# Weights taken with a step of two, moving columns and PSUM bank run through backwards, in a graph-convolution and LSTM kernel

## The reference

```
h   = item_feat @ W_item.T + b_item                 # 10000 x 128
b   = layernorm(x) @ W_user.T + b_user
x1  = x + relu(adj @ h + b)                          # adj is 10000 x 10000, fp32
y   = lstm(layernorm(x1))                            # 10000 steps, hidden size 128
out = x1 + 2*y + prefix*fw_att + suffix*bw_att       # running sums of y gated by a two-way logit
```

## Time and profile before

| | us |
|---|---|
| median of 3 runs | 1426.8 (1426.69 to 1429.94) |
| the profiled execution | 1429.61 |
| its span, first to last instruction | 1427.8 |
| stage one, block 0 (first pass to tail pass) | 10.0 to 86.9 |
| stage one, blocks 1 to 19 | 86.9 to 1125.8 |

### The profile page before, as it was taken

How to read it: one execution, slowest core, us unless ns; L and a number is a source line. 1 busy time by engine, 2 the same in 40 slices (tenths; PEclk the granted TensorE clock), 3 DMA queues, 4 the chain that set the end, 5 groups by cost and what they waited for, 6 DMA issues and landing times.

```text
span 1427.8 us, 26195 instructions
## 1 busy us (share of the span) xinstructions
PE 1401.8 (98%) x7438; PEld 1210.5 (85%) x7438; DVE 1273.0 (89%) x2102; ACT 1056.4 (74%) x1449; POOL 213.4 (15%) x189
## 2 busy tenths in 40 slices
PE   8999999999999999999999999999999999999995
PEld 7888888888888888888888888888888899999995
DVE  7999999999999999999999999999999766676667
ACT  5677787777877877877877877877877676556663
POOL 0000000001001001001001001001000132036776
PEclk9999999999999999999999999999999999999998
DMA  9999999999999999999999999999999303000003
GB/s 373 344 336 382 399 387 392 394 385 383 405 385 395 391 387 397 392 382 402 384 387 402 391 377 405 387 380 402 388 388 382 133 1 144 0 2 0 0 0 145
DMA packets 143466, 442.96 MB, mean 310 GB/s; under 512 B 23944, under 2 KB 43337, under 8 KB 143307
## 3 DMA queue, kind: packets, MB, share of 16 engines
q1 hardware_dynamic: 126048, 426.43, 76.7%
q10 hardware_dynamic: 17387, 16.14, 4.0%
HBM read 432.15 MB, written 10.36 MB: 310 GB/s over the span
## 4 chain that ended last, share of the span: by engine, by line
PE 93%; DVE 5%; ACT 0%; issue 0%; DMA 0%; POOL 0%; ACTq 0%; DVEq 0%
PE psG L882 24%; PE psG L883 24%; PE psG L884 24%; PE psZ L980 10%; PE psZ L966 3%; PE psZ L968 3%; PE psZ L970 3%; DVE a_lo L1201 2%; PE psZ L986 1%; PE psT L857 1%; PE psI L930 1%; DVE item_lo L1234 1%; DVE u L1516 1%; DVE u L1215 0%; PE psG L875 0%
## 5 line engine op out<-in xcount | busy, mean ns | idle before, releaser
L665 ACT ACTIVATE a_hi<-raw 128x1000 fp32r<-128x1000 f32 (+1 forms) x800 | 819.5, 1030 | 241.9 <-PE psG L884 212.7
L1201 DVE TENSOR_TENSOR a_lo<-raw,a_hi 128x1000 fp32r<-128x1000 f32 (+1 forms) x800 | 897.8, 1171 | 22.9 <-ACT a_hi L665 19.9
L882 PE MATMUL psG<-a_hi,item_hi 128*128 128x500 f32 x1560 | 611.3, 392 | 2.3 <-DVE a_lo L1201 1.4
L883 PE MATMUL psG<-a_lo,item_hi 128*128 128x500 f32 x1560 | 606.0, 388 | 0.0
L884 PE MATMUL psG<-a_hi,item_lo 128*128 128x500 f32 x1560 | 604.6, 388 | 0.0
L882 PEld LDWEIGHTS psG<-a_hi,item_hi 128*128 128x128 f32 x1560 | 293.5, 188 | 65.5 <-DVE a_lo L1201 3.5
L884 PEld LDWEIGHTS psG<-a_hi,item_lo 128*128 128x128 f32 x1560 | 293.1, 188 | 59.5
L883 PEld LDWEIGHTS psG<-a_lo,item_hi 128*128 128x128 f32 x1560 | 293.7, 188 | 55.5
L980 PE MATMUL psZ<-hist,wh 128*128 (+1 forms) x1264 | 167.1, 275 | 2.9 <-DVE hist L1354 2.2
L980 PEld LDWEIGHTS psZ<-hist,wh 128*128 128x128 f32 x1264 | 154.0, 191 | 3.8 <-issue 2.4
L466 POOL TENSOR_TENSOR row_terms<-var,minus_half 125x4 f32<-125x4 f32 x20 | 37.6, 1878 | 677.9 <-DVE var L1152 677.9
(11 more groups left out here) (186 smaller groups left out, 857.1 us busy)
## 6 DMA issues: line engine op xcount, KB each, us to landing
raw<-in_adj_main SPq DMA_DIRECT2D x760, 500.0 KB, 6.6
raw<-in_adj_main SPq DMA_DIRECT2D x40, 250.0 KB, 4.7
sq<-rstd_copy ACTq DMA_DIRECT2D x20, 250.0 KB, 7.0
u<-x_copy SPq DMA_DIRECT2D x1, 5000.0 KB, 14.4
x_copy<-x_rows SPq DMA_DIRECT2D x19, 250.0 KB, 7.2
sq<-rows_copy ACTq DMA_DIRECT2D x19, 250.0 KB, 5.3
un_bb<-rows_copy ACTq DMA_DIRECT2D x19, 250.0 KB, 7.6
u<-in_itemT SPq DMA_DIRECT2D x9, 512.0 KB, 8.0
```

The lines of the kernel that those rows point to most:

```text
L665: nc.scalar.activation(a_hi[:, s % CUT, 0:n], raw[:, r % RAW, at:at + n], ACT.Copy)\
L882: pe.matmul(bank, w_hi, hi, start=(c == 0), stop=False)
L883: pe.matmul(bank, w_hi, lo, start=False, stop=False)
L1201: last = dve.tensor_tensor(a_lo[:, s % CUT, 0:m], raw[:, r % RAW, at:at + m], a_hi[:, s % CUT, 0:m].bitcast(f32), ALU.subtract)
```

## The change

The item parts are stored in pairs of chunks: in each 256 columns the even ones belong to the first chunk, the odd ones to the second, so that a chunk's weights are 128 columns with a step of two. The item matmul L930 writes `psI` in that order, and the bias `bi` is doubled (each element twice), so that the elementwise steps stay as wide as they were. The passes of L882 to L884 read their moving slices from the last column to the first and write the bank from the last column to the first; L875 and the three bias passes stay forwards. The room for the wider `bi` comes from `inv_rows` and `item_tail`, which become parts of `x1_rows`, and five small tiles (`moments`, `mean_sum`, `mean_gap`, `gap_sq`, `spread`) stand between the large ones. Worked out as above, `item_hi` stays at 69440, `item_lo` comes to 110016, `a_hi` to 182560 and `a_lo` to 198560. Stage two is untouched.

```diff
+PAIR = 2 * HID
...
-        inv_rows = sb("inv_rows", [2, P])
...
-        bi = sb("bi", [P, HID])
+        bi = sb("bi", [P, 2 * HID])
...
         item_hi = sb("item_hi", [P, (CH + 1) * HID], f32r, first)
-        item_tail = sb("item_tail", [P, STACKED], f32, first)
+        moments = sb("moments", [SW, SUB, 6], f32, first)
+        mean_sum = sb("mean_sum", [SW, SUB], f32, first)
         item_lo = sb("item_lo", [P, (CH + 1) * HID], f32r, first)
         raw = sb("raw", [P, RAW, MAXC * BW], f32, first)
+        mean_gap = sb("mean_gap", [SW, SUB], f32, first)
+        gap_sq = sb("gap_sq", [SW, SUB], f32, first)
+        spread = sb("spread", [SW, SUB], f32, first)
...
+        item_tail = x1_rows[:, 2 * HID:2 * HID + STACKED]
+        inv_rows = x1_rows[0:2, 3 * HID:4 * HID]
...
+        def item_cols(c):
+
+            return slice(c // 2 * PAIR + c % 2, (c // 2 + 1) * PAIR, 2) if c < CH else slice(c * HID, (c + 1) * HID)
...
                 bank = psG[:, par, 0:BW]
+                back = bank[:, ::-1]
...
-                            hi = a_hi[:, s % CUT, i * BW:(i + 1) * BW]
-                            lo = a_lo[:, s % CUT, i * BW:(i + 1) * BW]
-                            w_hi = item_hi[:, c * HID:(c + 1) * HID]
-                            w_lo = item_lo[:, c * HID:(c + 1) * HID]
-                            pe.matmul(bank, w_hi, hi, start=(c == 0), stop=False)
-                            pe.matmul(bank, w_hi, lo, start=False, stop=False)
-                            last = pe.matmul(bank, w_lo, hi, start=False, stop=False)
+                            hi = a_hi[:, s % CUT, i * BW:(i + 1) * BW][:, ::-1]
+                            lo = a_lo[:, s % CUT, i * BW:(i + 1) * BW][:, ::-1]
+                            w_hi = item_hi[:, item_cols(c)]
+                            w_lo = item_lo[:, item_cols(c)]
+                            pe.matmul(back, w_hi, hi, start=(c == 0), stop=False)
+                            pe.matmul(back, w_hi, lo, start=False, stop=False)
+                            last = pe.matmul(back, w_lo, hi, start=False, stop=False)
...
+            def quad_cols(c):
+                k = c % 4
+                return slice(k // 2 * PAIR + k % 2, (k // 2 + 1) * PAIR, 2) if c < CH else slice(k * HID, (k + 1) * HID)
...
-                    last = pe.matmul(psI[0:rows, q % 2, (c % 4) * HID:(c % 4 + 1) * HID], columns, wi[:, :],
+                    last = pe.matmul(psI[0:rows, q % 2, :][:, quad_cols(c)], columns, wi[:, :],
...
-                                      bi[:, :].unsqueeze(1).to_broadcast([P, n, HID]), ALU.add)\
+                                      bi[:, :].unsqueeze(1).to_broadcast([P, n // 2, PAIR]), ALU.add)\
...
-            dve.tensor_copy(bi[:, :], psW[:, 0:HID]).then_inc(bi_ready, 1)
+            dve.tensor_copy(bi[:, :].rearrange("p (h e) -> p h e", e=2),
+                            psW[:, 0:HID].unsqueeze(2).to_broadcast([P, HID, 2])).then_inc(bi_ready, 1)
```

More of the change, by code:

```diff
@@ L35 @@
 STACKED = STACK[-1] + TAIL
+PAIR = 2 * HID
+assert CH % 2 == 0
 PIECES = 20
@@ L143, in program @@
         total = sb("total", [P, 1])
-        wd, dfd = wi, bi
+        wd, dfd = wi, bi[:, 0:HID]
         first = ExitStack()
         item_hi = sb("item_hi", [P, (CH + 1) * HID], f32r, first)
-        item_tail = sb("item_tail", [P, STACKED], f32, first)
+        moments = sb("moments", [SW, SUB, 6], f32, first)
+        mean_sum = sb("mean_sum", [SW, SUB], f32, first)
         item_lo = sb("item_lo", [P, (CH + 1) * HID], f32r, first)
         raw = sb("raw", [P, RAW, MAXC * BW], f32, first)
+        mean_gap = sb("mean_gap", [SW, SUB], f32, first)
+        gap_sq = sb("gap_sq", [SW, SUB], f32, first)
+        spread = sb("spread", [SW, SUB], f32, first)
         a_hi = sb("a_hi", [P, CUT, HALF * BW], f32r, first)
@@ L166, in program @@
         v = un_bb[:, 0:BW]
[L167 to L171, removed]
         var = sb("var", [SW, SUB], f32, first)
@@ L874, in body @@
                             if c == CH:
-                                last = pe.matmul(bank, item_hi[0:STACKED, c * HID:(c + 1) * HID],
+                                last = pe.matmul(bank, item_hi[0:STACKED, item_cols(c)],
                                                  a_hi[0:STACKED, s % CUT, i * BW:(i + 1) * BW], start=False, stop=True)
                                 continue
-                            hi = a_hi[:, s % CUT, i * BW:(i + 1) * BW]
-                            lo = a_lo[:, s % CUT, i * BW:(i + 1) * BW]
-                            w_hi = item_hi[:, c * HID:(c + 1) * HID]
-                            w_lo = item_lo[:, c * HID:(c + 1) * HID]
-                            pe.matmul(bank, w_hi, hi, start=(c == 0), stop=False)
-                            pe.matmul(bank, w_hi, lo, start=False, stop=False)
-                            last = pe.matmul(bank, w_lo, hi, start=False, stop=False)
+                            hi = a_hi[:, s % CUT, i * BW:(i + 1) * BW][:, ::-1]
[5 more added lines that the diff above has]
+                            last = pe.matmul(back, w_lo, hi, start=False, stop=False)
                         last.then_inc(halves_done, 1)
@@ L1214, in item_sum_part @@
                     dst = u[:, L + 4 * q * P:L + (4 * q + n) * P]
-                    dve.tensor_tensor(dst.rearrange("p (c h) -> p c h", h=HID),
-                                      psI[:, q % 2, 0:n * HID].rearrange("p (c h) -> p c h", h=HID),
-                                      bi[:, :].unsqueeze(1).to_broadcast([P, n, HID]), ALU.add)\
+                    dve.tensor_tensor(dst.rearrange("p (c h) -> p c h", h=PAIR),
+                                      psI[:, q % 2, 0:n * HID].rearrange("p (c h) -> p c h", h=PAIR),
+                                      bi[:, :].unsqueeze(1).to_broadcast([P, n // 2, PAIR]), ALU.add)\
                         .then_inc(item_sum, 1)
@@ L1222, in item_sum_part @@
                 dve.wait_ge(prep, 1)
[L1223 to L1226, removed]
+                pair, single = slice(0, PAIR), slice(PAIR, PAIR + HID)
+                for part, a, b in ((pair, 0, P), *((single, a, a + TAIL) for a in STACK)):
+                    dve.tensor_tensor(sq[a:b, part], psI[a:b, q % 2, part],
+                                      bi[a:b, :] if part is pair else bi[a:b, 0:PAIR:2], ALU.add)\
                         .then_inc(item_sum if a == STACK[-1] else prep, 1)
```

## The result

The change makes the kernel slower: 1438.55 us median (1437.33 to 1439.22, 4 runs) against 1427.6 for the kernel before beside it (4 runs), ratio 1.0075 with a 95% interval of 1.0061 to 1.0089, some 11 us. The prediction of 1404 had it faster, and the result lies outside its range. The profiled execution took 1437.87, its span is 1436.1, 8.3 more than before.

The account below looks back on a forecast made before the run. The prediction took TensorE to bound the blocks, with VectorE and DMA within 5%. Blocks 1 to 19 at -25 us and block 0 at +2 on a span of 1427.8 gave 1404.8, so a median of 1404; range 1380 to 1430.

Parts of the forecast that it names:

- Side by side they should meet once and part: Stage one's passes: weight and slice reads, both running downwards at one speed, would meet once, cutting 226.5 ns to 213.
- the 213 ns: Predicted time of a stage-one pass after the change, from 226.5, with 208 as the lower bound; TensorE needs 51.4 us a block.
- it comes once per pass: Claim that a TensorE pass's loss, 18 ns at 500 columns, comes once per pass, as the weight load does.
- hardly grows with the columns: Claim on TensorE passes: the loss is 12 ns at stage two's 256 columns and 18 ns at stage one's 500.
- Rival A: Stage one's passes stay as they are, so only block 0's +2 us remains: 1427 to 1429 us; chance 0.17.
- Rival C: Stage one's weight loads with a step of two take longer: passes some 246 or 300 ns, +93 or +350 us; chance 0.17.
- the 38 to spare: Slack in ns of a stage-one weight load: it lasts 188 within a pass of 226.5, and beyond that it decides.
- stage two 0: Stage two keeps its code and addresses, so its time was to change by 0.
- bound 0.3: Copy to the doubled `bi`, on the path of the first quad in block 0: at most +0.3 us.
- low end of its bounds: Block 0's step-two writes of `psI` by the item matmul: bounds 0 and +21 us, taken as +4.
- the DMA as the next bound: Blocks 1 to 19, once passes are faster: DMA sets 53.3 us a block, 1.3 less, -25 us over 19 blocks.
- floors of 52.6 to 54.2: DMA time per block, in us, behind the forecast's own span of 1392 to 1419 us; chance 0.52.

Follow-up runs that it names:

- e5: Kernel of TensorE passes alone with other lengths, a repeated column and 64 pairs of weight and slice places: 13 pairs settle at 220.0 ns, the rest at 223 to 229.
- e4: Kernel of TensorE passes alone, tiles at the addresses of the kernel before, 48 passes per form: 226.0 ns as before, 228.6 as after.
- e6: Passes alone, one weight place and 16 slice places, for backwards, step two and both: none settles at 220 ns; backwards 226.7 at 11 of 16.
- e11: e10 with the slices and the bank of the three passes run through backwards: 1432.41 us, ratio 1.0025.
- e8: The kernel before with 384 of 500 columns in the passes of L882 to L884, all but a block's first: 1404.3 us, blocks of 53.41 us.
- e9: Passes alone at the addresses of e7, 48, then other passes or nothing, then 48 more: 220 ns with nothing between, 226 to 233 after one of 64 columns.
- e2: The changed kernel with slices and bank forwards again, step of two and new tile places kept: 1433.15 us, ratio 1.0035.
- e1: The kernel before with only the slices and the bank of the three passes run through backwards: 1441.36 us, ratio 1.0099.
- e7: The kernel before with slices padded to 512 columns and tiles moved so each slice starts 64 bytes after each item weight, mod 128: 1431.5 us, ratio 1.0019.
- e3: The kernel before with the tiles at the addresses of the changed kernel and nothing else: 1427.24 us, ratio 0.9998.
- e10: e7 with small tiles moved so the bias weights and `v_hi`, `v_lo` also stand 64 bytes apart, mod 128: 1417.19 us, ratio 0.992.

## Why the prediction was wrong

- **The step that failed** is "Side by side they should meet once and part", and with it the 213 ns. No pass of the changed kernel is under 224; the mean went from 225.7 to 228.0. That the loss goes by the addresses of both reads was right as far as the runs go (e5), and it is TensorE's own (e4). That equal direction and speed would part the reads was only argued, and the runs show the reverse: of the four forms, forwards with a step of one is the only one that settled at 220 anywhere, and backwards or with a step of two the means stayed at 226 or more (e6, e11). Before, a fifth of the starts (869 of some 4300) were 219 to 222; the changed kernel has none. Their loss is some 6 of the 10 us; for the rest, the other starts went from 227.2 to 228.0. The rest of the forecast for the blocks stood: e8, with TensorE made fast in another way, gave 1404.3.
- **A step under it** was wrong as well: "it comes once per pass" and "hardly grows with the columns". It is 11 ns at 256 columns and 18 at 500. The prediction had 12 against 18 in its own rows and called that hardly any growth; besides, are of other weights and tiles, and two lengths from unlike places can't give a slope. That at the lower clock nothing is lost held: 415 to 419 in e9's start.
- **Rival A** had the right reason ("rows 8 show that place matters, not that direction does") but not the price: the passes did not stay as they were. The stated range ended 8.5 us short of the result because neither A nor C had a term for passes that lose their cheap places. The spread in the earlier trace rows, 382 against 393, was the sign of it: where passes sit on two levels, a change can lose the lower one as well as gain it.
- **Rival C** has its mechanism and not its price: loads with a step of two last 6 ns longer (194 against 188), far inside the 38 to spare; the step costs about 1 ns a pass in e2 and e4. Its form with a step of four is near what I had priced: loads of 318, but passes of 235.5, not 300, so a long load does not decide the pass in the way I had put it. The Trainium skill's two uses of a 16-byte line (SBUF — State Buffer, in its box on cachelines) fit the small cost of step two and the jump at four for the weights. They do not fit the moving slice: with a step of two it takes 443 ns (e5, the last rows below).
- **The rule of the Trainium skill** that TensorE's two reads wait on no one (SBUF — State Buffer, "Who interferes with whom") is not borne out: e5 moves the weights by 16 to 64 bytes, and the same slice (`a_lo` from its first column) goes from 220.0 to 223 or more. The Trainium skill's rule on non-contiguous banks (PSUM — Partial Sum Buffer, "Specifications (TRN2)") is not seen either: bank backwards 225.8 against 226.0, and L941's eight writes in 1.05 us, those at half the full pace.
- **What held**: stage two 0; `bi` +0.13 us (bound 0.3); L941 at the low end of its bounds, 0, not +4; the DMA as the next bound at 53.3 us a block, which e8 puts at 53.41, with ScalarE waiting for `raw` and a rate of 402 GB/s. That it was 53.3 and not 52.2 or 54.6 was a middle taken between two bounds, so the closeness is in part luck.
- **Slips in the sum**, too small to matter: the middle of 52.2 and 54.6 is 53.4; a mean block of 54.7 less 53.3 gives 26 us over 19 blocks, not 25; and floors of 52.6 to 54.2 give 1391 to 1421, not 1392 to 1419.
- **Block 0** ended 2.1 us earlier, which I had at +2. It is no part of the change's work: e1 and e7 show the early end (84.8, 84.6), e2, e3, e10 and e11 the late one (86.5 to 87.0). In the kernel before the passes start 417 ns apart, the pace of the lower clock, until 12.3 us; in the changed one they start 225 to 230 apart from 10.2 us on, so the clock rose earlier there (the clock column of the rows has 1.00 for both). Why is open, and so it is luck that took 2 us off the slowdown. The row is of the changed kernel, then of the one before:

```profile
10.00:13.00 3.00, 3.00 (x18) 2.69 (x19) 2.08 (x3) 2.10 (x3) 0.00 (x0) 1.00 0.97 355
```

```profile
10.00:13.00 3.00, 2.97 (x8) 2.45 (x9) 1.69 (x2) 1.62 (x2) 0.00 (x0) 1.00 0.97 354
```

**Open**: what inside TensorE makes the two rhythms, why a backward moving read never reached the fast one, and why four passes of 128 columns end the slow one in e7 and not in e9, no run shows. Nor was it tried to bring the last slow stretches of e10 to 220.

## What to carry to other kernels

Where TensorE is the bound, read the distance between starts place by place, not the mean. Two levels at like instructions (here 220 and 226 to 233) mean that addresses or what came before matter, and a change can lose the low level as easily as win it. A belief about how two streams meet should be priced in both directions; a kernel of passes alone, 248 us long here, was enough to show that this one was wrong. Padding slices and moving small tiles, so that every slice stands at one good distance from every weight tile, was worth 11 us here once the three bias passes were included (e10); without them it cost 3 us (e7). Turning the streams round cost 14 us (e1).

## What was not expected of the hardware

- A pass of 500 fp32r columns has two steady rhythms at the same addresses, 220.0 ns flat and a turn of six with a mean of 228.7, and in e7 it stays in the one that it entered for a hundred passes and more. In e9 a single pass of 64 columns behind the bias passes brought the slow one and one of 256 columns the fast one.
- Read backwards, a pass costs 226.7 at 11 of 16 places (e6), and in e11 behind transposes and bias passes alike.
- A moving slice with a step of two takes 443 ns, twice a contiguous one. Weights with a step of 4, 8 and 16 load in 318, 336 and 302 ns and cost 235.5, 245.1 and 231.9 a pass.

The load and the pass of e5 with the moving step of two, by line:

```profile
L114 PEld LDWEIGHTS psG<-a_hi,item_hi x16: 189/207/209, 140.3 to 160.0; 128*128 128x128 f32 x16
L114 PE MATMUL psG<-a_hi,item_hi x16: 616/625/628, 140.5 to 160.4; 128*128 128x500 f32 x16
```
